# A decoder layer on one core: the Out product of cross-attention over 28 tiles of 128 rows instead of 32 of 112

## What is computed

```python
q = input_seq @ Wq.T + bq;  k = ctx @ Wk.T + bk;  v = ctx @ Wv.T + bv
attn = softmax(einsum('bse,bte->bst', q, k))
attended = einsum('bst,bte->bse', attn, v)
x = layernorm(x + attended)
```

## Time and profile before

| what | us |
|---|---|
| median of 3 runs | 1410.64 (1409.54 to 1412.51) |
| the profiled execution's own time | 1409.47 |
| its span, first to last instruction | 1407.5 |
| cross-attention's steps 1 to 16 on TensorE | about 388 to 830 |
| one steady step | 28.51 |

### The profile page before, as it was taken

The page is one execution under the profiler, slowest core; times in us unless marked ns, Lnnn a source line. Parts: engine busy times, 40 slices in busy tenths (PEclk is TensorE's granted clock), DMA queues, the critical chain, the costliest instruction groups (busy, mean ns, idle before and its releaser), DMA issues.

```text
span 1407.5 us, 28532 instructions
## 1 busy us (share of the span) xinstructions
PE 1381.1 (98%) x10017; PEld 1208.2 (86%) x10017; DVE 922.0 (66%) x1911; ACT 733.0 (52%) x1989; POOL 570.2 (41%) x475
## 2 busy tenths in 40 slices
PE   7999999999999999999999999999999999999997
PEld 3677777777899999999999988999999999999775
DVE  4589999999667667765777673345443454536687
ACT  4588888888565666566655554222222222322232
POOL 2567767776575656656565620000000000010264
PEclk9999999999999999999999999999999999999999
DMA  7114322336386877676769553011010100000353
GB/s 213 39 43 107 105 81 76 104 105 172 100 230 192 223 201 214 172 230 195 218 178 266 157 156 100 0 27 26 0 27 0 26 13 20 30 1 31 105 186 122
DMA packets 133463, 157.94 MB, mean 112 GB/s; under 512 B 62688, under 2 KB 70880, under 8 KB 133392
## 3 DMA queue, kind: packets, MB, share of 16 engines
q1 hardware_dynamic: 133392, 157.01, 39.7%
HBM read 105.61 MB, written 35.78 MB: 100 GB/s over the span
## 4 chain that ended last, share of the span: by engine, by line
PE 65%; issue 3%; POOL 2%; DVE 2%; ACT 0%; DMA 0%; POOLq 0%; DVEq 0%; ACTq 0%
PE banks L1528 16%; PE banks L1557 11%; PE banks L1023 9%; PE banks L1007 9%; PE banks L1036 6%; PE banks L1559 6%; PE banks L992 5%; PE banks L977 1%; POOL o_r L2103 1%; PE banks L1989 1%; PE banks L1053 1%; POOL o_rstd L2111 1%; DVE s_dot L1222 1%; PE banks L2020 0%; DMA x_scratch<-a_xn 0%
## 5 line engine op out<-in xcount | busy, mean ns | idle before, releaser
L461 ACT ACTIVATE s_p<-banks,a_nmax 112x224 f32<-112x224 f32 (+1 forms) x512 | 198.5, 413 | 58.3 <-DVE a_nmax L572 58.2
L759 POOL TENSOR_TENSOR s_p<-s_p,a_rinv 112x896 f32<-112x896 f32 (+1 forms) x128 | 164.7, 1308 | 116.7 <-DVE a_rinv L580 113.6
L1502 POOL CAST m_hi<-w_raw 128x2048 fp32r<-128x2048 f32 x1 | 2.3, 2267 | 407.8 <-PE banks L1528 407.8
L1645 ACT ACTIVATE f_gate<-f_gate 128x448 f32<-128x448 f32 x90 | 52.2, 580 | 198.5 <-DVE f_gate L1768 198.5
L1765 DVE TENSOR_TENSOR f_gate<-banks,f_xg_early 128x448 f32<-128x448 f32 x45 | 28.1, 624 | 189.6 <-PE banks L1559 189.6
L1369 POOL TENSOR_TENSOR x_cx_lo<-s_cx_raw,x_cx_hi 125x512 fp32r<-125x512 f32 x96 | 121.3, 1301 | 31.1 <-ACT x_cx_hi L1136 31.0
L571 DVE TENSOR_REDUCE a_nmax<-banks 112x1 f32<-112x224 f32 x256 | 97.8, 382 | 23.2 <-PE banks L277 22.4
L461 ACT ACTIVATION_READ_ACCUMULATOR s_p<-banks,a_nmax 112x1 f32 x512 | 111.7, 218 | 0.0
L294 PEld LDWEIGHTS banks<-identity,s_p 112*112 112x112 f32 x768 | 87.7, 134 | 21.6 <-issue 2.1
L294 PE MATMUL banks<-identity,s_p 112*112 112x112 f32 x768 | 105.0, 260 | 1.2 <-POOL s_p L759 0.7
L1362 POOL TENSOR_TENSOR s_ct<-s_ct_raw,s_ct 128x750 fp32r<-128x750 f32 x60 | 98.5, 1676 | 0.2 <-ACT s_ct L1111 0.2
(11 more groups left out here) (255 smaller groups left out, 3720.4 us busy)
## 6 DMA issues: line engine op xcount, KB each, us to landing
s_ct_raw<-in_ct SPq DMA_DIRECT2D x16, 1500.0 KB, 6.7
s_cx_raw<-in_cx SPq DMA_DIRECT2D x16, 1344.0 KB
a_xt<-in_xt SPq DMA_DIRECT2D x16, 448.0 KB, 6.2
a_xrow<-in_x SPq DMA_DIRECT2D x16, 448.0 KB, 5.7
a_xres<-in_x SPq DMA_DIRECT2D x16, 448.0 KB, 6.4
x_scratch<-a_xn SPq DMA_DIRECT2D x16, 448.0 KB, 3.3
x_scratch<-x_xn SPq DMA_DIRECT2D x16, 448.0 KB, 4.6
x_halves<-x_halves SPq DMA_DIRECT2D x16, 448.0 KB, 3.1
```

The costliest lines, as they stand in the source:

```text
L461: e = act.activation((p1 if c else p0)[:, g, h, :], src, ACT.Exp, bias=nmax[:, g % 2, c, h:h + 1], accum_out=rsum[:, g % 2, c, h:h + 1])
L759: pool.tensor_tensor(p[:, g, :, :], p[:, g, :, :], inv, ALU.mult).then_inc(norm_done, 1)
```

## The change

Four sequences are 896 rows, which are 7 tiles of 128. Out, the residual, the statistics, the norm and the stores now go by such tiles. Within each four sequences the first finishes one tile and the other three two each (`OF`); rows that don't fill a tile stay in `ot_hi` and `ot_lo` until the next sequence brings the rest (`SLOT`, `PUT`), so that the evacuation of the second and fourth sequence is cut into two pieces per bank. Scores, softmax, P and O stay as they were.

As the residual's rows now lie in other partitions than the softmax's, the inverse row sums can't be used in place. They are stored to DRAM as 4-byte values (`rinv_scratch`) and read back by tile (`rinv_rows`). The rows of x1 for the residual are loaded by tile as well (`x1b`), one buffer instead of two, and GpSimd adds bv in place; it does so behind `power` instead of ahead of `ctl`. The dot product takes its rows from `ahead`, one sequence earlier than before, so that the load of the next rows into `ahead` waits for `rowbias_done`. In steps with a single tile ScalarE rounds `x1t_hi` between the two exponentials. The loops go over four steps instead of two.

```diff
+        OF = ((0, 1), (1, 3), (3, 5), (5, 7))
+        SLOT = ((0,), (1, 2), (0, 1), (2, 0))
+        PUT = (((0, T, 0),), ((0, 160, T), (160, T, 0)), ((0, T, 64),), ((0, 96, 288), (96, T, 0)))
...
+            def inverse_rows(b, at, odd):
+                wait(sp, rinv_stored, 16 * (b + 1))
+                    sp.dma_start(rinv_rows[:, odd, 0:rows(at)], rinv_dram[i][128 * OF[q][0]:128 * OF[q][1]].rearrange("(n p) -> p n", p=128))\
+            def residual_rows(b, at):
+                wait(sp, rinv_done, b + 1)
+                    sp.dma_start(rinv_scratch[b].rearrange("(c p) -> p c", p=R), rinv[:]).then_inc(rinv_stored, 16)
+                wait(sp, r_done, TC * b)
+                sp.dma_start(x1b[:, 0:rows(at), :], tiles_of(x1_rows, at)).then_inc(x1b_in, 16)
...
-                if within(b + 1, B):
-                    load_rows(b + 1, 1 - odd)
+                if within(b - 2, B):
+                    inverse_rows(b - 2, (i, q - 2), odd)
...
                 if isinstance(b, int) and b == 1:
                     sp.wait_ge(shared.stored, 16 * B)
+                    sp.wait_ge(ahead_stored, 16)
+                    sp.wait_ge(rowbias_done, 3)
+                    rows_ahead(3)
                 elif within(b + 1, B):
...
+                        wait(sp, rowbias_done, b + 2)
                         rows_ahead(b + 2)
+                residual_rows(b - 1, (i, q - 1))
...
-                        for k in range(KC):
-                            mm = pe.matmul(ps_h[0:R, c, :], y[:, k, c * R:c * R + R], w[:, k, :],
+                            mm = pe.matmul(ps_h[:, c, :], y[:, k, slot], w[:, k, :], start=(i == 0), stop=(i == 3 * KC - 1))
...
                 wait(dve, x1b_done, b + 1)
+                wait(dve, rinv_in, 16 * (b + 1))
+                    dve.scalar_tensor_tensor(out=r[:, c, :], in0=ps_h[:, c, :], scalar=rinv_rows[:, q % 2, c:c + 1], in1=x1b[:, c, :],
...
+                if isinstance(b, int) and b == 1:
+                    dve.wait_ge(rowbias_done, 2)
+                    row_bias(2, 0)
```

More of the change, by code:

```diff
@@ L921, in loads @@
+            def loads(b, odd, at=None):
+                i, q = four(b if at is None else at)
                 if not (isinstance(b, int) and b == 1):
@@ L948, in sync @@
                 loads(b, b % 2)
[L949 to L952 removed]
+            with sp.Fori(1, B // 4 - 1) as i:
+                for q in range(4):
+                    loads(4 * i + q, q % 2, (i, q))
+            for b in range(B - 4, B - 1):
+                loads(b, b % 2)
             for i, name in enumerate(("wi_t", "wf_t")):
@@ L1026, in s, with out @@
                     mm.then_inc(s_done, 1)
-            def out(b, rows=range(TC)):
-                if rows[0] == 0:
+            def out(b, at, some=range(TC)):
+                _, q = four(at)
+                n = len(SLOT[q])
+                if some[0] == 0:
                     wait(pe, otl_done, b + 1)
                     wait(pe, ztl_done, min(b + 2, B) if isinstance(b, int) else b + 2)
-                for c in rows:
+                for c in some[0:n]:
+                    slot = slice(128 * SLOT[q][c], 128 * SLOT[q][c] + 128)
                     i = 0
@@ L1129, in oth @@
                     wait(act, ot_done, 2 * b + half + 1)
-                    act.activation(ot_hi[:, 2 * half:2 * half + 2, :], ps_g[:, half, 0:2 * T], ACT.Copy).then_inc(oth_done, 1)
+                    for first, end, place in PUT[q]:
+                        a = act.activation(ot_hi[:, 2 * half:2 * half + 2, place:place + end - first], ot_columns(half, first, end), ACT.Copy)
+                    a.then_inc(oth_done, 1)
             def cxh(b):
@@ L1240, in ztl, with otl @@
                 q.then_inc(ztl_done, 1)
-            def otl(b, halves_of=range(2)):
+            def otl(b, at, halves_of=range(2)):
                 for half in halves_of:
                     wait(dve, oth_done, 2 * b + half + 1)
-                    q = dve.tensor_tensor(ot_lo[:, 2 * half:2 * half + 2, :], ps_g[:, half, 0:2 * T], ot_hi[:, 2 * half:2 * half + 2, :], ALU.subtract)
+                    for first, end, place in PUT[four(at)[1]]:
+                        to = slice(place, place + end - first)
+                        low = dve.tensor_tensor(ot_lo[:, 2 * half:2 * half + 2, to], ot_columns(half, first, end),
+                                                ot_hi[:, 2 * half:2 * half + 2, to], ALU.subtract)
                 if half == 1:
-                    q.then_inc(otl_done, 1)
+                    low.then_inc(otl_done, 1)
             def row_max(b):
@@ L1268, in statistics @@
+            def statistics(b, at):
+                n = rows(at)
+                each = TC // n
+                for c in range(n):
+                    wait(dve, r_done, TC * b + each * (c + 1))
+                    dve.bn_stats(stats[:, c, :], r[:, c, :]).then_inc(stats_done, each)
+                for c in range(n):
                     dve.wait_ge(pad_done, 1)
-                    wait(dve, stats_done, TC * b + c + 1)
-                    dve.bn_aggr(mv[:, c, :], stats[:, c, :]).then_inc(mv_done, 1)
```

314 lines of the change are left out of this document (171 added, 143 removed).

## The result

The changed kernel takes 1434.63 us (median of 4, 1431.39 to 1438.08) against 1410.66 (1409.54 to 1412.51) before, a ratio of 1.0168 [1.0151, 1.0185]. It is slower by 24.0 us where 5.6 us of gain were predicted. The profiled execution has a span of 1432.0 us, 24.5 more than before.

The account below looks back on a forecast made before the run. TensorE, 98% full, was taken as the bound. Three single-tile steps save 8.4 us, their transposes return 0.5, the start-up loses 2.3: 5.6 us off 1410.6 gives 1405.0, range 1401.6 to 1410.0.

Parts of the forecast that it names:

- The sums' way through DRAM: Store and read of the sums, per sequence: in at 577 to 580, hidden by at least 3 us.
- Rival (b): Cross-attention: sums' read back lands late behind context and transposing load, residual holds Z product; about 1439 us, chance 0.07.
- Matmuls removed: Out in cross-attention: 32 tiles become 28, 2.80 us each, 11.2 us for four; wider tiles cost nothing more.
- Steps 5, 9, 13: Single-tile steps: 2.80 us saved each, 0.17 given back at the transposes; nothing for `x1t`, up to 0.8 in the range.
- The start-up: Steps 1 and 2: queue tied to row biases, Z product of sequence 2 at 417.6, loss 2.3 us (0.7 to 4.8).
- the two paths in the prediction: Start-up, to sequence 2's Z product: `x1t` rounded and split by 416.9; sums in at 416.3 to 417.1, then residual.
- The end: Step 15 and closing stage: later transposing loads covered, last rows of x1 after the residual; 0, up to 1 us.
- The sum: Whole kernel: -8.4 for three steps, +0.5 transposes, +2.3 start-up: -5.6 us, from 1410.6 to 1405.0.
- Rival (c): VectorE's norm waits behind back-to-back GpSimd work, evacuation late for Out: 13 steps, +39 us, 1444; chance 0.04.
- The chance for "slower": Whole kernel: 0.11 that it measures slower, against faster 0.70 and same 0.19.

Follow-up runs that it names:

- run 13: The whole change with the inverse sums 512 bytes apart in DRAM, for store and read back, against the kernel before: 1404.51 us, ratio 0.9963.
- run 14: The whole change with sums 512 bytes apart, and rows ahead of sequence 3 loaded behind the first transposing load, against the kernel before: 1402.39 us, 0.9952.
- run 5: The kernel before plus a store of 112 pieces of 4 bytes side by side, in front of the context's columns, never read: 1419.5 us.
- run 1: The kernel before plus the store of the inverse sums, 224 pieces of 4 bytes side by side, never read back: 1416.97 us, ratio 1.0050.

## Why the prediction was wrong

**The step that failed** is "The sums' way through DRAM". It priced the read back from the earlier trace rows and gave the store its issue and nothing more. The ends of its range came from loads; no row of before shows a store of small pieces, and the step didn't say so. Rival (b) had the symptom, a slow small transfer, but on the read, which was on time at 3.1 us. The kernel's own store took 9.7 us and put some 6 on every load behind it. With only the spacing changed, 30 us of it are gone (1434.6 to 1404.5).

**How the 24.5 us come about.** Starts of the transposes of P, which open a step, in the two traces:

| stretch | before | expected | after | with spacing (13) |
|---|---|---|---|---|
| to the start of step 1 | 388.18 | 388.18 | 389.01 | 389.05 |
| steps 1 and 2 | 54.80 | 57.1 | 66.10 | 59.40 |
| steps 3 and 4 | 57.11 | 57.1 | 57.01 | 57.01 |
| steps 5 to 14 | 285.2 | 277.3 | 298.5 | 277.3 |
| of these, step 5 | 28.53 | 25.9 | 30.26 | 25.85 |

The end is 0.8 us shorter after (see below), which makes 24.5. Against the expected 277.3, steps 5 to 14 lost 21.2.

- *Matmuls removed*: right. 336 of 128 columns at 0.23 us, and 25.85, 25.86 and 25.76 us for the single-tile steps of run 13.
- *Steps 5, 9, 13*: the prediction let `x1t` land at 578.6 against ScalarE's gap from 579.0 and counted nothing for it. The order was the risk it took: rounding stands ahead of the second exponential, so a late `x1t` holds that up, and TensorE with it. After, around the start of step 6, ScalarE and TensorE:

```profile
539.86 0.95 ACT L1149 ACTIVATE x_x1t_hi<-s_x1t 128x896 fp32r<-128x896 f32 x1 [5.36 <-DMA s_x1t<-x_halves]
...
541.36 0.89 ACT L1206 ACTIVATE x_p<-banks,x_shift 112x750 f32<-112x750 f32 x1
```
```profile
542.38 2.86 PE L1023 MATMUL banks<-identity,x_p 112*125 112x112 f32 x12 [3.91 <-ACT x_p L1206]
```

  This is why the steps that should have saved 2.6 us each lost 1.7, 1.1 and 0.9 (5, 9 and 13). The three stops of TensorE, 3.91, 2.53 and 3.54 us, are 10.0 of the 21.2. Another 7.9 lie in steps 6, 10 and 14, which have no wait of their own and take 31.85, 31.60 and 30.24 us where run 13 has 28.6: behind each stop the granted clock was 0.50. Waits for the residual are 2.5; 0.8 stay open. With the spacing the term is right: nothing for the wait, 0.1 to 0.2 for the transposes.
- *The start-up*: the moment was right, its price not. In run 13, where the store is cheap, the Z product of sequence 2 comes at 418.61, 417.7 with the trace's lag of 0.87 taken off; predicted 417.6. That it fits so well is partly luck. The sums, the later of the two paths in the prediction, were in at 415.5. The other path decided: VectorE's split of `x1t` took 1.52 us, not 1.09, until 417.80, and the residual, which the prediction didn't add to this path, stands behind it until 418.47. And steps 1 and 2 cost 4.6 us more than before, not 2.3. The other 2.2 are the clock. Around that wait in run 13 (the columns are engines' busy us, then the granted clock, DMA share, GB/s):

```profile
414.00:416.00 2.00, 1.59 (x13) 1.39 (x12) 0.00 (x0) 0.70 (x1) 2.00 (x3) 1.00 0.40 81
416.00:418.00 2.00, 0.00 (x0) 0.00 (x0) 1.72 (x2) 2.00 (x3) 2.00 (x2) 0.79 0.02 4
418.00:420.00 2.00, 1.39 (x6) 1.42 (x7) 2.00 (x5) 2.00 (x6) 0.94 (x1) 0.50 0.04 6
420.00:422.00 2.00, 2.00 (x11) 2.00 (x11) 1.97 (x4) 2.00 (x4) 1.86 (x1) 0.50 0.88 172
422.00:424.00 2.00, 2.00 (x11) 2.00 (x11) 1.96 (x3) 0.22 (x1) 2.00 (x2) 0.50 1.07 296
424.00:426.00 2.00, 2.00 (x20) 2.00 (x19) 1.33 (x4) 0.00 (x0) 2.00 (x2) 1.00 1.06 272
```

  TensorE stood still for 3.0 us, its clock fell to 0.50 (1.2 GHz), and from there to the next step it takes 29.84 us where it took 27.64. The Z product alone takes 8.00 us where it took 5.43. In run 14, with a stop of 1.15 us and a clock of 1.00 behind it, it takes 27.27.
- *The end*: predicted 0; from step 15 to the end run 13 is 1.4 us shorter. Of this 1.0 us is a wait in the closing stage for a load of rows, 1.5 us before and 0.5 in run 13 (0.4 after). Why that load is in sooner isn't shown. The wait before:

```profile
PE banks L1971 <- DMA s_o_x_a<-x_scratch: 1.5, 1, 1.5
```

- *The sum*: run 13 confirms the mechanism of the prediction, but its total only in part. Its trace is 3.9 us shorter than that of before and its median 5.9 us lower than the 1410.42 measured beside it; the predicted 5.6 lies between. The start-up (2.3 us dearer than predicted, and 0.9 of lag) and the end (1.4 shorter) miss in opposite directions.
- *Rival (c)*: didn't happen; no list of TensorE's waits that was read has one for the norm, and the longest norm of the changed kernel took 3.0 us. *The chance for "slower"*, 0.11, named two mechanisms on reads and ports and left none for an operation that the trace of before doesn't have.

## What to carry to other kernels

Price every new transfer in the direction in which it goes and in the shape of its pieces; a load is no bound for a store. Here one value from each partition, written side by side in DRAM, made the loads behind it 6 us late; a 512-byte spacing of the scratch (1404.51) or a transposed row (1404.56) removed that. When a queue's order is changed, ask of each load what a doubled landing would hold up: here two instructions exchanged on ScalarE let a late `x1t` stop TensorE.

## What the runs showed of the hardware

- 112 or 224 pieces of 4 bytes, stored side by side, delay the transfers of both queues tried (`x1t` by 6.3 to 6.8 us from SyncE's, by 4.1 from ScalarE's). Set 16 bytes apart they hardly do (0.9 us on `x1t`), 512 apart not to speak of (0.4). From the fifth to the eleventh store of run 5 the landing takes 6.0, 7.8, 6.8, 8.2, 6.1, 8.3 and 6.2 us. That might be the place in DRAM or anything else that alternates with the sequence; no run tells them apart, and run 1 doesn't alternate so.
- 4-byte *reads* of the same kind land after 3 to 4 us, and the result's store behind them in the queue isn't late (3.6 us in the changed kernel, 4.6 before).
- Stops of 2.5 to 3.9 us on TensorE cost more than themselves, by the clock that was low behind them: 2.2 us more in run 13, and 3.2, 3.0 and 1.6 us behind the stops of 3.91, 2.53 and 3.54 us in the changed kernel. Behind its stops of 1.2 and 1.0 us, at 605.4 and 635.2, the matmuls ran as before (0.71 and 0.68 us for four of the Z product, against 1.16 behind the stop of 11.27). Behind the stop of 3.91 us at 542.38 the transposes took 2.86 us instead of 1.56 (columns as above):

```profile
542.00:544.00 2.00, 1.62 (x8) 1.62 (x8) 0.67 (x2) 2.00 (x3) 0.00 (x0) 0.59 0.95 228
544.00:546.00 2.00, 2.00 (x11) 2.00 (x11) 1.29 (x3) 1.72 (x5) 0.00 (x0) 0.50 1.02 323
546.00:548.00 2.00, 2.00 (x11) 2.00 (x11) 1.97 (x4) 2.00 (x4) 1.38 (x1) 0.50 1.09 234
```
